# Both value products of a key pair in one unit instead of two, in an attention and mixture-of-experts block

## The reference

```python
q, k, v = split(layernorm(x) @ qkv_w.T + qkv_b)          # 8 heads of 24
attn = softmax(l2norm(q) @ l2norm(k).T * temperature)    # 1024 x 1024 for each head
x = x + (attn @ v) @ proj_w.T + proj_b
t = tokens(x); n = layernorm(t)
gates = top 2 of softmax(n @ gate_w + gate_b), renormalised
t = t + sum_e gates[e] * (gelu(n @ w1[e] + b1[e]) @ w2[e] + b2[e])
```

## The kernel before, in words

| units | jobs |
|---|---|
| 2 to 5 | one x in each |
| 6 to 9 | x in 6, 7, 8; none in 9 |
| 10 to 13 | n in 13 |
| 14 to 17 | 14 u; 15 v; 16 n |
| 18 to 21 | 18 r; 19 u a; 20 v a; 21 n |
| 22 to 25 | 22 b; 23 u; 24 v q a; 25 n |
| 26 to 29 | 26 b; 28 u c; 29 v q |
| 30 to 33 | 30 n a; 32 u b; 33 v q |
| 34 to 37 | 34 n c; 36 a; 37 u |
| 38 to 41 | 38 v q b; 39 n; 40 c; 41 u a |
| 42 to 45 | 42 v q; 43 n b; 45 c |
| 46 to 49 | 46 u; 47 v q a; 49 b |
| 50 to 53 | 51 q c; 53 a |
| 54 to 57 | 55 b; 56 q; 57 c |
| 58 to 61 | 59 b; 61 c |
| 62 to 1 | 63 c; 1 x |

## Time and profile before

### The profile page before, as it was taken

How to read it: one execution, slowest core, us unless ns; L and a number is a source line. 1 busy time by engine, 2 the same in 40 slices (tenths; PEclk the granted TensorE clock), 3 DMA queues, 4 the chain that set the end, 5 groups by cost and what they waited for, 6 DMA issues and landing times. The chain is left out here.

```text
span 2557.4 us, 57736 instructions
## 1 busy us (share of the span) xinstructions
PE 2368.7 (93%) x20228; PEld 1451.7 (57%) x20228; DVE 1681.7 (66%) x4966; ACT 1889.6 (74%) x2967; POOL 1424.5 (56%) x1511
## 2 busy tenths in 40 slices
PE   3799999999999999999999975899999999999997
PEld 2334334334334433433433322799999999999887
DVE  4657678767867867876786765555656565566553
ACT  3487887788788788778778853677777777777775
POOL 3334446535535544643553523577777777777775
PEclk9799999999999999999999988899999999999999
DMA  4221222222112112222211343788788887888775
GB/s 80 62 51 39 50 62 51 51 51 62 49 44 61 51 46 67 51 51 51 59 49 33 78 130 102 293 295 299 292 323 321 313 306 291 323 319 311 288 296 201
DMA packets 174131, 380.64 MB, mean 149 GB/s; under 512 B 23220, under 2 KB 140676, under 8 KB 156180
## 3 DMA queue, kind: packets, MB, share of 16 engines
q1 hardware_dynamic: 155876, 349.55, 41.4%
q0 software_dynamic: 12912, 26.99, 3.0%
q10 hardware_dynamic: 5056, 0.42, 0.3%
HBM read 279.41 MB, written 47.48 MB: 128 GB/s over the span
## 5 line engine op out<-in xcount | busy, mean ns | idle before, releaser
L825 ACT ACTIVATE probs<-ps_s 128x1024 f32<-128x1024 f32 x1024 | 1008.3, 1023 | 210.1 <-PE ps_s L718 206.9
L1458 POOL TENSOR_TENSOR h_split<-h_f,h_split 128x256 f16<-128x256 f32 x828 | 562.6, 692 | 217.8 <-ACT h_f L1431 214.6
L1377 PE MATMUL ps_h<-m_xn_t,packs 128*128 128x256 f16 x4140 | 588.0, 273 | 4.7 <-DMA packs<-expert_pack 3.0
L1427 ACT ACTIVATE h_split<-ps_h,packs 128x256 f16<-128x256 f32 x828 | 392.9, 475 | 240.7 <-PE ps_h L1377 240.1
L731 PE MATMUL ps_o<-probs,v_aug 128*32 128x512 f32 x4096 | 547.0, 606 | 1.1 <-DVE o_sb L851 0.7
L1391 PE MATMUL ps_y<-packs,h_split 128*128 128x192 f16 x4968 | 544.9, 246 | 2.1 <-POOL h_split L1458 2.1
L1103 POOL TENSOR_TENSOR inv_norm<-sumsq,minus_half 128x16 f32<-128x16 f32 x128 | 380.5, 2972 | 273.9 <-DVE sumsq L1046 273.6
L1391 PEld LDWEIGHTS ps_y<-packs,h_split 128*128 128x128 f16 x4968 | 434.9, 97 | 21.6 <-POOL h_split L1458 3.0
L1377 PEld LDWEIGHTS ps_h<-m_xn_t,packs 128*128 128x128 f16 x4140 | 389.7, 98 | 36.4 <-issue 5.3
L1431 ACT ACTIVATE h_f<-ps_h,packs 128x256 f32<-128x256 f32 x828 | 386.7, 467 | 0.0
L718 PE MATMUL ps_s<-even 98*128 98x512 f16 x1024 | 300.2, 383 | 12.8 <-ACT probs L825 11.0
(11 more groups left out here) (224 smaller groups left out, 2802.4 us busy)
## 6 DMA issues: line engine op xcount, KB each, us to landing
packs<-expert_pack SPq DMA_DIRECT2D x138, 1635.0 KB, 8.7
even<-heads SPq DMA_DIRECT2D x192, 96.0 KB, 2.4
stacks_odd<-heads SPq DMA_DIRECT2D x192, 96.0 KB, 2.4
tile_rows<-sorted_rows SPq DMA_DIRECT2D x69, 200.0 KB
tokens<-in_x_dram SPq DMA_DIRECT2D x16, 768.0 KB, 5.5
y_in<-y_tokens SPq DMA_DIRECT2D x15, 768.0 KB, 4.4
out_dram<-y_out SPq DMA_DIRECT2D x15, 768.0 KB, 11.4
even<-heads SPq DMA_DIRECT2D x128, 48.0 KB
```

The source lines that it names most:

```text
L825: act.activation(probs[:, u % PRING, :], ps_s[:, u % 2, :, :].rearrange("p f n -> p (f n)"), ACT.Exp).then_inc(s_probs, 1)
L1377: mm = pe.matmul(ps_h[:, (STEPS * tile + n) % HBUF, 0:TROWS], w1(par, slot, w, k), xn_t[0:rows_k, par, c, :], start=(i == 0), stop=(i == 4))
L1427: act.activation(h_split[:, (STEPS * tile + n) % HSPLIT, 0, :], ps_h[:, (STEPS * tile + n) % HBUF, 0:TROWS], ACT.Gelu, bias=bias1(par, slo ...
L1458: pool.tensor_tensor(h_split[:, (STEPS * tile + n) % HSPLIT, 1, :], h_f32[:, (STEPS * tile + n) % HBUF, :], h_split[:, (STEPS * tile + n) ...
```

## The change

`PV_UNITS` holds one unit for each group, 4p+6, and `pe_image` issues both `pv` of the group there, one right behind the other, between the scores and the jobs of that unit. No instruction is added, removed or resized. Relative to before, the first `pv` of three groups in four is one unit later (4p+5 to 4p+6), and the second `pv` of every group is one unit earlier (4p+7 to 4p+6). The wait of `pv` for `s_probs` stands, as before, ahead of the first of the two only.

```diff
-PV_UNITS = [GH * p + at for p in range(UNITS // GH) for at in ((6, 7) if p % (PHASE // GH) == 0 else (5, 7))]
+PV_UNITS = [GH * p + 6 for p in range(UNITS // GH)]
...
-            if u in PV_UNITS and attend:
-                pv(pe, img, par, PV_UNITS.index(u))
-            elif u + UNITS in PV_UNITS and has_post(img):
-                pv(pe, img - 1, 1 - par, PV_UNITS.index(u + UNITS))
+            for i in range(2):
+                if u in PV_UNITS and attend:
+                    pv(pe, img, par, 2 * PV_UNITS.index(u) + i)
+                elif u + UNITS in PV_UNITS and has_post(img):
+                    pv(pe, img - 1, 1 - par, 2 * PV_UNITS.index(u + UNITS) + i)
```

## The result

The changed kernel takes 2628.02 us (median of four runs, 2627.74 to 2630.87) against 2557.23 us for the kernel before, measured alongside: a ratio of 1.0272, 95% interval 1.026 to 1.0284. It is slower by 71 us. The profiled execution has a span of 2626.3 us, 68.9 more than before.

What follows compares the result with a forecast made beforehand. PE sets the pace but is tied to ACT by two score buffers, whose path lengthens blocks: +44.8 us in fourteen images, +5.1 in image 0, +4.9 in image 15, +55 in all, giving 2612 us, range 2577 to 2632.

Steps and rivals of the forecast that it cites:

- the rival in which DVE's and GpSimd's delay carries on past unit 25: Units 26 to 37 keep 18.16 us, 38 to 45 gain 0.5 more waits, image 15 shows its 4: 2630 us; chance 0.15.
- What comes off PE: Two adjacent value products cost PE 1.94 us instead of 2.16 for two lone ones: 0.22 saved a pair, 256 pairs.
- The block rule H + 2.63: Four units from 4p+6 take at least first unit H plus 0.63, 0.92 and 1.08 us through ACT, plus copies between.
- blocks 38 and 42: Attention blocks from units 38 and 42, with ACT's q and n copies: 7.02 us each, together 14.04, before 13.47.
- Units 54 to 65: Three light attention blocks, from units 54, 58 and 62: 5.01 us each, together 15.03, before 15.44.
- The first blocks: Attention blocks from units 2, 6 and 10: 5.23, 5.23 and 5.01 us, together 15.47, before 14.03.
- blocks 46 and 50: Attention blocks from units 46 and 50: 6.70 and 5.91 us, together 12.61, before 10.95.
- Units 18 to 25: r issued behind the pair makes DVE's list start later: 14.2 us, before 13.84; least trusted term, 11.9 to 14.8.
- Units 26 to 37: Blocks from units 26, 30 and 34: 5.96, 5.98 and 5.74 us, together 17.68, before 18.16.
- Image 1: Lacks r but taken like a steady image: 94.8 us against 91.6, +3.2.
- Image 15: Lengthening up to unit 33 hidden by DVE and weight loads, otherwise +4; from unit 34 39.6 us against 34.7, +4.9.
- The faster rival: PE alone sets the pace, so 256 savings of 0.22 us come off: 2501 us, 56 less; chance 0.05.

Runs made afterwards that it cites:

- the pair kept apart: The changed kernel with the jobs of unit 4p+6 placed between its two value products, so not adjacent where the unit has jobs: 2643.98 us.
- the gain with four buffers: Both orders with exponentials of half length and four score buffers instead of two: 2527.87 us for the old order, 2513.01 for the new.
- The run with r first: The changed kernel with the jobs ahead of the pair in units 18 and 30 only: 2625.93 us.
- the one attempt to space it more evenly: The kernel before with value products in units 5 and 7 in place of 6 and 7 for the first and fourth phase: 2557.94 us, ratio 0.9989.
- the kernel with units 6 and 7: The kernel before with every group's two value products in units 4p+6 and 4p+7, PE's own work unchanged: 2618.4 us, ratio 1.0228.

## Why the prediction was right, and where not

It gave 2612 us, 2577 to 2632, and slower at 0.90; 2628 lies inside. The sum was +55, the spans say +68.9. The direction and its mechanism are right. The size is right only by the wider range: 2628 is above the forecast's own 2600 to 2622 and stands next to the 2630 of the rival in which DVE's and GpSimd's delay carries on past unit 25. Of that rival one part in three came: units 26 to 37 took 18.32, and its 18.16 is nearer than my 17.68, but by DVE's list and not by GpSimd; units 38 to 45 took no more than forecast, and image 15 didn't show its 4 us.

- **What comes off PE** (0.22 a pair): right, 0.24 by the pair kept apart, and by the gain with four buffers. By Key Properties of TensorEngine Tiling (Array Packing) in the Trainium skill changing the mode drains the engine; the runs show no drain as such, but they agree that a change costs time, and put 0.24 us on two changes.
- **The block rule H + 2.63**, with its copies of q and n: right, to 0.03 us in the light blocks and 0.07 in blocks 38 and 42. Units 54 to 65 took 15.09 against 15.03. The first blocks took 15.50 against 15.47, blocks 38 and 42 13.90 against 14.04, blocks 46 and 50 12.63 against 12.61.
- **Units 18 to 25**: the number was right (14.25 against 14.2), its reason wrong. I put DVE's lag down to r, issued behind the pair. DVE in fact runs without a hole from unit 15's v into r, and its list is late since then: that v now follows the pair and unit 14's u, and its evacuation starts 4.28 us after unit 14 does instead of 3.80 (783.20 - 778.92 in the changed kernel, 751.14 - 747.34 before). The prediction has nothing of that lateness; that r, ready at 2.65 us by my reckoning, was taken up at 2.68 is luck. The run with r first shows r innocent; that unit 15 is the origin is read from the traces and was not tried alone.
- **Units 26 to 37**: the step that failed, 17.68 against 18.32. All of it is block 30, 6.60 instead of 5.98. The q of unit 33 waits 0.6 us for its bank, the one that unit 32's u was in: DVE takes out that u only at 810.54, at the end of a list without a hole that begins with the a of unit 30, and the a stands behind the pair. The timeline of DVE in the changed kernel, the first line 2.99 us into unit 30:

```profile
807.92 0.21 DVE L881 RECIPROCAL o_rec<-ps_m 128x8 f32<-128x8 f32 x1 [0.78 <-PE ps_m L780]
...
810.54 0.45 DVE L870 SCALAR_TENSOR_TENSOR heads<-ps_m,bias_qkv 128x288 f32<-128x288 f32 x1
```

  I had counted PE's stall at that a as hidden, which it is, and forgot what stands behind the a on DVE. With the a ahead of the pair the q no longer waited, which bears this out. Over 13 images this is 8 of the 14 us missing.
- **Image 1**, +7.1 instead of +3.2: 1.6 of it is a clock dip in block 26 (7.60 us instead of 5.97). The rest is that this image, which lacks r, was 1.7 us shorter than a steady one before the change, and without the dip would be about as long as one now (95.4).
- **Image 15**: the 1.2 us before unit 34, at a granted clock of 0.88 in both kernels, fit what I said, that most of the 4 is hidden. The last part was 41.0 instead of 39.6, since block 34 ran at a granted clock of 0.76, as its window in the changed kernel says:

```profile
1586.27:1592.81 6.54, 5.55 (x26) 1.17 (x24) 3.16 (x15) 3.02 (x4) 0.33 (x1) 0.76 0.01 3
```

- **The faster rival** had the saving right and the buffers wrong: with four, and exponentials of half the length, its direction holds, but 15 us came of its 56.

No version that leaves nothing out beat the kernel before by more than the noise. The old order, with a value product in every second unit, keeps ACT fed; the one attempt to space it more evenly brought nothing.

## What to carry to other kernels

When a producer feeds another engine through two buffers, read the cycle through the handshake as well as the busy shares: the longest stretch in which the producer makes nothing, plus start-up, plus the consumer's steps until the buffer comes free. Here it predicted light blocks to 0.03 us, while an engine at 96% busy suggested that saving its work must help. Batching work to save mode changes pays only if the buffers cover the longer batch. And where a step is moved, follow what stands behind its consumer in that engine's list, not only the consumer.

## What the runs showed of the hardware that was not expected

The granted clock can fall in the midst of attention, close behind small idle stretches. In the kernel with units 6 and 7, PE is idle 0.47 and 1.15 us in units 24 and 25, and then the granted clock falls to one half (1.2 GHz) for 3 us; one `pv` that takes 1.06 us of busy span takes 1.94:

```profile
790.52 0.44 PE L780 MATMUL ps_m<-ident,o_sb 128*128 128x128 f32 x2 [0.47 <-DVE heads L869]
...
792.54 0.34 PE L762 MATMUL ps_m<-ident,xn_split 128*128 128x128 f16 x3 [1.15 <-DVE heads L876]
...
793.53 1.94 PE L731 MATMUL ps_o<-probs,v_aug 128*32 128x512 f32 x8
```

The windows there (the clock is the third number from the end):

```profile
789.00:793.00 4.00, 2.38 (x22) 1.46 (x20) 3.10 (x12) 3.15 (x4) 3.50 (x3) 0.99 0.06 22
793.00:796.00 3.00, 3.00 (x14) 0.65 (x13) 1.96 (x6) 1.43 (x2) 2.67 (x4) 0.50 0.23 78
```

It costs block 26 1.6 us each time. The gaps alone don't decide it: the six images of this kernel without a dip have the same two gaps within 0.05 us, and the changed kernel has gaps of 0.64 and 1.15 us (1.10 in image 1) in these units of its images and dips there only in image 1. The kernel before has the first gap, but not the long one (0.16 us at most), and no dip in images 1 to 14. What decides was not tried.
